# An AdaLN block on one core: both ends reworked, the modulation rows after the first projection, and a key-value product in halves

## The chip, the core and the metric

One core of a Trainium2 chip runs the whole program. The metric is device time in microseconds (us), lower is better. In the text TensorE does matmuls (PE in the profile, PEld for its weight loads), VectorE is DVE, ScalarE is ACT, GpSimd is POOL, and SyncE (SP) issues most of the DMA transfers. Each engine runs its own instructions in order and waits on semaphores.

## The reference

x is 2 x 2048 tokens of 256 values; c holds one conditioning row for each of the two batches.

```python
mod = (silu(c) @ wmod).reshape(2, 6, 1, 256)
sa, ca, ga, sb, cb, gb = (mod[:, i] for i in range(6))
ga = (2 * (ga >= 0) - 1) * maximum(abs(ga), 0.25)     # gb alike
h = layernorm(x) * (1 + ca) + sa
x = x + ga * linear_attention(h)     # 16 heads of 16: Q, K = elu(.) + 1
h = layernorm(x) * (1 + cb) + sb
x = x + gb * moe(h)                  # 8 experts, 256 -> 128 -> 256, gelu, top 2
```

Linear attention is Q (K^T V) / (Q sum K), then the output projection Wo and its bias bo. The router adds a cosine score to a linear one. All is fp32.

## The kernel before

Tokens are worked in 16 units (NU) of two tiles of 128 tokens; eight units make a batch. Two pipelines run over the units, each a `step_a` or `step_e` on every engine, with the same semaphores counted per unit.

**Attention pass (`step_a`).** VectorE makes the layer norm statistics (`stats_a`, three units ahead), GpSimd the reciprocal root (`rstd_a`), ScalarE normalises, TensorE transposes (`tp_a`, L720), ScalarE modulates by columns, VectorE rounds to the high half (`split_a`, L1052), GpSimd makes the low half (`split_lo`, L376). TensorE projects in three products of halves: `qk` (bias L739, then L708 to L710) for each tile, then `v`. ScalarE and VectorE form the feature map (`feature_map`, L1134), and TensorE adds K^T V for the unit before (`kv`, L774): for each half c of the 256 features a 128 x 128 fp32 product, of which only the 16 x 16 blocks of a head on the diagonal are used. VectorE adds it to `kv_acc` (`add_kv`, L1145). GpSimd sums K (`add_ksum`) and adds ga * bo to x (`add_bo`, L393). VectorE also splits a sixteenth of the expert weights in each unit (`split_weights`).

**Start.** Eight matmuls on TensorE (L793) give the modulation columns sa and ca. `mod_rows(b)` then gives ga, sb, cb, gb of batch b as rows spread over all 128 partitions, by a weight operand `c_rep` in which silu(c) is repeated 128 times: four fp32 matmuls of 512 columns, recorded as eight. Batch 0 comes ahead of the first projection, batch 1 after it. VectorE's `mod_rows(b)` clips the two gates (ten operations, L1100 to L1116), and `bias_o` forms ga * bo. On GpSimd, the centroid norm (`normalise_centroids`, L520) stands between the steps of unit 0 and 1, and needs VectorE's `clip_centroids`, which follows `mod_rows(1)`. SyncE issues all loads of x, W and small rows in one queue; from unit 4 on the x loads wait for the load two units before.

**Middle.** After eight units of a batch `mask_kv` (L1197, L1202) adds the value bias and masks K^T V to its diagonal blocks, `make_m` (L837) folds it into Wo, and `split_m` multiplies by ga. The expert pass starts while the last units of attention end.

**Expert pass (`step_e`).** For each unit four expert pairs p: TensorE `first(u, p)`, ScalarE gelu, VectorE `gate(u, p)` (L1279), ScalarE the high half (`hi_hid`, L664), GpSimd the low half (`lo_e`), or VectorE (`lo_hid`, L1286) in the last two units; then TensorE `second(u, p)` (its first instruction for p = 0 is L918) sums into bank 6. VectorE's `scale_experts(u)` (L1343) empties that bank, and the next unit's `second(u, 0)` waits for it (`e_yg`). In `step_e(u)` VectorE runs, in order, gate 0, 1, 2, then `scale_experts(u - 1)`, then gate 3. In the last unit, tile 1 sums into bank 7.

## Time and profile before

| | us |
|---|---|
| median of 3 runs (388.28 to 390.07) | 389.62 |
| the profiled execution | 390.11 |
| its span, first to last instruction | 388.40 |

| engine | busy us | share |
|---|---|---|
| TensorE | 355.6 | 92% |
| TensorE weight loads | 331.6 | 85% |
| VectorE | 294.5 | 76% |
| ScalarE | 229.2 | 59% |
| GpSimd | 283.7 | 73% |

The page cuts the span into 40 slices of 9.7 us. A digit is the busy share in tenths; PEclk is the clock granted to TensorE in tenths of full speed.

```profile
PE   4897999999997655999999999999999999999696
DVE  4889777777886877787887887887887887776443
POOL 3716899999976758689888888888888888765201
PEclk9999999999999966799999999999999999999899
```

A timeline row is: start in us from the span's start, duration, engine, line, operation, output<-inputs, shape, count, and in brackets the idle time of the engine before it and what ended that. Rows with a count over 1 are several instructions merged. Matmul ends are modelled, so that neighbouring durations overlap; from one start to the next is the better measure.

### The profile page before, as it was taken

The page shows a single profiled execution, that of the slowest core. Times are in us where ns is not written, and L with a number is a line of the kernel's source. Part 1 is how long each engine was busy: PE and PEld are TensorE (multiplying, and loading weights), DVE is VectorE, ACT ScalarE, POOL GpSimd, SP SyncE. Part 2 cuts the span into 40 slices and gives each one's busy share as a digit, 9 for nine tenths or more (in the row PEclk, how much of TensorE's full clock was granted, in tenths as well). Part 3 has the DMA queues.
Part 4 walks back from the last instruction along what each step waited for, and adds up shares of the span by engine and source line. Part 5 has one row for each costly group of instructions (what it writes and reads, how often), then busy time and mean ns, then how long its engine had stood idle before and what let it go on. Part 6 is the DMA issues. An engine that isn't in the chain of part 4 may idle for free.

```text
span 388.4 us, 8954 instructions
## 1 busy us (share of the span) xinstructions
PE 355.6 (92%) x2610; PEld 331.6 (85%) x2610; DVE 294.5 (76%) x833; ACT 229.2 (59%) x499; POOL 283.7 (73%) x389
## 2 busy tenths in 40 slices
PE   4897999999997655999999999999999999999696
PEld 4376889888896644999999999999999999999685
DVE  4889777777886877787887887887887887776443
ACT  2245778778773414765855855855855855773450
POOL 3716899999976758689888888888888888765201
PEclk9999999999999966799999999999999999999899
DMA  7954000000000002203224214214214214233301
GB/s 260 336 175 155 2 0 0 0 0 0 2 1 0 2 16 93 83 32 136 84 57 136 82 55 135 82 55 135 82 55 135 82 56 135 84 88 105 131 7 56
DMA packets 23147, 30.35 MB, mean 78 GB/s; under 512 B 2242, under 2 KB 13906, under 8 KB 23124
## 3 DMA queue, kind: packets, MB, share of 16 engines
q1 hardware_dynamic: 22308, 29.02, 23.8%
q10 hardware_dynamic: 816, 1.05, 0.8%
q8 instruction: 11, 0.18, 0.2%
q14 instruction: 12, 0.10, 0.1%
HBM read 25.74 MB, written 4.33 MB: 77 GB/s over the span
## 4 chain that ended last, share of the span: by engine, by line
PE 56%; POOL 7%; DVE 6%; issue 4%; ACT 2%; POOLq 0%; DVEq 0%
PE bank L708 17%; PE bank L710 16%; PE bank L709 16%; PE bank L716 3%; PE bank L880 2%; POOL x_sb L393 1%; PE bank L918 1%; POOL k_sum L386 1%; DVE hid_g L1279 1%; POOL tr_lo L376 1%; ACT hid_pair L664 1%; POOL early L424 1%; POOL early L434 1%; POOL rstd L360 1%; PE bank L837 1%
## 5 line engine op out<-in xcount | busy, mean ns | idle before, releaser
L657 ACT ACTIVATE bank<-bank,cols_sb 128x256 f32<-128x256 f32 x128 | 51.4, 439 | 50.6 <-PE bank L710 50.5
L461 POOL TENSOR_TENSOR hid_pair<-hid_g,hid_pair 128x512 fp32r<-128x512 f32 x56 | 72.4, 1293 | 6.9 <-ACT hid_pair L664 4.6
L708 PE MATMUL bank<-tr_hi,w_hi 128*128 128x256 f32 x256 | 74.4, 290 | 0.0
L710 PE MATMUL bank<-tr_hi,w_lo 128*128 128x256 f32 x256 | 72.9, 285 | 0.0
L709 PE MATMUL bank<-tr_lo,w_hi 128*128 128x256 f32 x256 | 72.8, 284 | 0.0
L708 PE MATMUL bank<-w_hi,hid_pair 128*128 128x256 f32 x252 | 70.9, 281 | 0.0
L709 PE MATMUL bank<-w_lo,hid_pair 128*128 128x256 f32 x252 | 70.9, 281 | 0.0
L710 PE MATMUL bank<-w_hi,hid_pair 128*128 128x256 f32 x252 | 70.9, 281 | 0.0
L664 ACT ACTIVATE hid_pair<-hid_g 128x512 fp32r<-128x512 f32 x64 | 40.4, 632 | 28.5 <-DVE hid_g L1279 27.1
L1279 DVE TENSOR_TENSOR hid_g<-bank,g_bc 128x512 f32<-128x512 f32 x64 | 43.7, 683 | 9.8 <-ACT bank L657 8.3
L708 PEld LDWEIGHTS bank<-tr_hi,w_hi 128*128 128x128 f32 x256 | 49.1, 192 | 0.2
L709 PEld LDWEIGHTS bank<-tr_lo,w_hi 128*128 128x128 f32 x256 | 49.1, 192 | 0.1
L710 PEld LDWEIGHTS bank<-tr_hi,w_lo 128*128 128x128 f32 x256 | 49.1, 192 | 0.0
L710 PEld LDWEIGHTS bank<-w_hi,hid_pair 128*128 128x128 f32 x252 | 48.2, 191 | 0.0
L709 PEld LDWEIGHTS bank<-w_lo,hid_pair 128*128 128x128 f32 x252 | 48.2, 191 | 0.0
L708 PEld LDWEIGHTS bank<-w_hi,hid_pair 128*128 128x128 f32 x252 | 48.1, 191 | 0.0
L710 PE MATMUL bank<-hid_pair,tr_lo 128*128 128x512 f32 (+1 forms) x128 | 43.7, 341 | 0.0
L708 PE MATMUL bank<-hid_pair,tr_hi 128*128 128x512 f32 (+1 forms) x128 | 43.5, 340 | 0.0
L709 PE MATMUL bank<-hid_pair,tr_hi 128*128 128x512 f32 (+1 forms) x128 | 43.5, 340 | 0.0
L577 ACT ACTIVATE e_sb<-bank 128x512 f32<-128x512 f32 x32 | 19.1, 597 | 27.3 <-PE bank L710 27.1
L1296 DVE STREAM_TRANSPOSE bank<-bank 32x64 f32<-32x64 f32 x64 | 16.6, 259 | 23.9 <-PE bank L880 23.2
L475 POOL TENSOR_TENSOR x_sb<-x_sb,k_sb 128x512 f32 (+1 forms) x15 | 19.6, 1303 | 16.6 <-DVE k_sb L1343 16.6
(152 smaller groups left out, 942.4 us busy)
## 6 DMA issues: line engine op xcount, KB each, us to landing
g_bc<-g_dram SPq DMA_DIRECT2D x64, 256.0 KB, 3.5
x_sb<-in_x SPq DMA_DIRECT2D x16, 256.0 KB, 2.9
out<-x_sb SPq DMA_DIRECT2D x15, 256.0 KB, 2.2
early<-in_wmod ACTq DMA_DIRECT2D x2, 512.0 KB, 8.1
q_sb<-in_w SPq DMA_DIRECT2D x2, 512.0 KB, 6.2
q_sb<-in_w SPq DMA_DIRECT2D x1, 1024.0 KB, 9.1
...
```

What stands on the lines that cost most here:

```text
L461: gp.tensor_tensor(hid_lo[:, p, :, :], hid_g[:, p % 2, :, :], hid_hi[:, p, :, :].bitcast(F32), ALU.subtract).then_inc(e_hlo, 1)
L475: gp.tensor_tensor(xt, xt, y_g[:, :, :], ALU.add).then_inc(e_y, 1)
L577: ac.activation(e_sb[:, t, :], bank[2 + t][:, :], ACT.Relu, scale=-1.0).then_inc(a_neg, 1)
L657: last = ac.activation(half, half, ACT.Gelu, bias=b1_sb[:, e:e + 1])
L664: ac.activation(hid_hi[:, p, :, :].rearrange("p j n -> p (j n)"), hid_g[:, p % 2, :, :].rearrange("p j n -> p (j n)"), ACT.Copy).then_inc( ...
L708: te.matmul(out_ap, l_hi, r_hi, start=start, stop=False, skip_group_check=shared)
L709: te.matmul(out_ap, l_hi, r_lo, start=False, stop=False, skip_group_check=shared)
L710: return te.matmul(out_ap, l_lo, r_hi, start=False, stop=stop, skip_group_check=shared)
L716: last = te.transpose(dst[:, c, t * P:(t + 1) * P], of[:, t, c * P:(c + 1) * P], ident[:, :])
L880: last = te.matmul(lgT, route_r[:, c, :], part[:, h, c, :], start=(c == 0 and k == 0), stop=(c == NC - 1 and k == 1))
L1279: TT(hid_g[:, s, :, :].rearrange("p j n -> p (j n)"), bank[2 + p][:, :], g_bc[:, p, :, :].rearrange("p j n -> p (j n)"), ALU.mult).then_in ...
L1296: last = ve.transpose(lg[32 * q:32 * (q + 1), :, :], by_quarter[:, :, q, :])
```

## The change

- **Modulation rows.** silu(c) itself, two columns, is the weight operand, so that both batches come at once in two partitions. `mod_rows(0)` and `mod_rows(1)` are now the two halves of the columns (ga, sb and cb, gb), both behind `step_a` of unit 0 on TensorE. VectorE clips the gates once, on two partitions, after its step of unit 0, and forms ga * bo there. SyncE waits for it, stores five rows of each batch to DRAM, waits, and reads them back to all partitions. GpSimd's first `add_bo` and VectorE's first `mask_kv` wait for that. TensorE's matmul for bo is gone.
- **Loads.** The last two parts of wmod are issued by SyncE ahead of x of unit 2; the small rows by ScalarE.
- **Who splits what.** The high half of Wq, Wk, Wv is made by ScalarE; the low half of unit 0 by VectorE; the bias rows are split by GpSimd (`split_bqk`), before the reciprocal root of unit 1.
- **GpSimd's order.** `normalise_centroids` comes after the step of unit 2. VectorE's `split_b2` and `split_route` move from unit 1 to unit 3.
- **Key-value product.** Only the two 64 x 64 blocks on the diagonal of each 128 x 128 are formed: eight matmuls of 64 weight columns by 64, in place of four of 128 by 128. `kv_acc` and the masking shrink to match; `kv_m` is cleared once.
- **End.** In the last two units `scale_experts(u - 1)` moves ahead of `gate(u, 2)`; the last unit sums into banks 0 and 7 and does not wait for `e_yg`.

The diff, without declarations:

```diff
@@ -252,7 +254,7 @@
 
         def sums(u, t):
 
-            return bank[7][:, 0:E] if t == 1 and u.nth(NU - 1) else bank[6][:, t * E:(t + 1) * E]
+            return bank[7 * t][:, 0:E] if u.nth(NU - 1) else bank[6][:, t * E:(t + 1) * E]
 
         def kv_bank(u):
             return bank[2] if u.nth(NU - 1) else bank[6 + u.h]
@@ -275,21 +277,28 @@
 
             x_tiles = x.rearrange("(t p) e -> p t e", p=P)
             out_tiles = out.rearrange("(t p) e -> p t e", p=P)
-            small = [(rows_raw[0:1, :], rows), (rows_raw[32:33, :], rows), (cols_sb[:, :], cols),
-                     (b2_raw[:, :], b2)]
-            assert len(small) == N_SMALL
+            def load_wmod(k):
+                cols_k = slice(k * 2 * E, (k + 1) * 2 * E)
+                sp.dma_start(wmod_sb[:, :, cols_k], wmod_chunks[:, :, cols_k]).then_inc(d_wmod[k], 16)
+
             load_x(0, 0)
-            sp.dma_start(wmod_sb[:, :, 0:2 * E], wmod_chunks[:, :, 0:2 * E]).then_inc(d_wmod[0], 16)
+            load_wmod(0)
             sp.dma_start(wqkv_raw[:, :, :], wqkvT.rearrange("(c p) n -> p c n", p=P)).then_inc(d_qkv, 16)
             load_x(0, 1)
-            for to, of in small:
-                sp.dma_start(to, of).then_inc(d_small, 16)
+            load_wmod(1)
+            load_wmod(2)
             load_x(1, 0)
             load_x(1, 1)
             sp.dma_start(w1_raw[:, 0, :, :], w1[:, 0:P, :].rearrange("e p j -> p e j")).then_inc(d_w, 16)
             sp.dma_start(w1_raw[:, 1, :, :], w1[:, P:2 * P, :].rearrange("e p j -> p e j")).then_inc(d_w, 16)
             sp.dma_start(w2_raw, w2.rearrange("e p d -> p e d")).then_inc(d_w, 16)
             sp.dma_start(wo_sb[:, :, :], woT.rearrange("(c p) n -> p c n", p=P)).then_inc(d_wo, 16)
+
+            sp.wait_ge(modrow_ready, 1)
+            sp.dma_start(mod_dram[:, 0:4, :], mod_of).then_inc(mod_put, 16)
+            sp.dma_start(mod_dram[:, 4, :], ga_bo).then_inc(mod_put, 16)
+            sp.wait_ge(mod_put, 32)
+            sp.dma_start(mod_row[:, :, :, :], mod_dram.partition_broadcast(P)).then_inc(mod_got, 16)
             with sp.Fori(2, NU // 2) as it:
                 for h in range(2):
@@ -402,14 +411,27 @@
                     add_ksum(u.plus(-1))
                 if u.nth(2):
 
-                    pool.wait_ge(ga_bo_ready, B)
+                    pool.wait_ge(mod_got, 16)
                 if u.plus(-2) and not u.plus(-2).nth(NU - 4) and not u.plus(-2).nth(NU - 3):
                     add_bo(u.plus(-2))
 
+            def split_bqk():
+
+                pool.wait_ge(d_small, 16 * N_SMALL)
+                pool.wait_ge(zero_rows, 1)
+                pool.wait_ge(a_rstd, 1)
+                gp.tensor_copy(bqk_t[32:33, :], bqk_raw[32:33, :]).then_inc(bqk_step, 1)
+                pool.wait_ge(bqk_step, 1)
+                gp.tensor_copy(bqk_r[0:1, :], bqk_raw[0:1, :]).then_inc(bqk_step, 1)
+                pool.wait_ge(bqk_step, 2)
+                gp.tensor_tensor(bqk_r[32:33, :], bqk_raw[32:33, :], bqk_t[32:33, :].bitcast(F32), ALU.subtract)\
+                  .then_inc(bqk_ready, 1)
+                pool.wait_ge(bqk_ready, 1)
+
             u0 = unit(0)
             rstd_a(u0)
+            split_bqk()
             rstd_a(u0.plus(1))
-            split_lo(u0)
 
             def make_prod(u):
 
@@ -520,8 +542,10 @@
                 gp.tensor_tensor(cent_rn[:, :], cent_n2[:, :], minus_half[:, :], ALU.pow).then_inc(cent_ready, 1)
 
             step_a(u0)
+            step_a(unit(1))
+            step_a(unit(2))
             normalise_centroids()
-            pipeline(gp, step_a, 1, 2, NU - 4, NU - 2)
+            pipeline(gp, step_a, 3, 4, NU - 4, NU - 2)
 
             pool.wait_ge(f_ksrow, 1)
             gp.memset(prod[:, :, D:D + 1], DEN_EPS)
@@ -548,9 +572,11 @@
 
             act.wait_ge(d_c, 16)
             ac.activation(c_exp[:, :, :], c_sb[:, :, :], ACT.Exp, scale=-1.0).then_inc(c_exp_ready, 1)
-            for k in range(1, 3):
-                cols_k = slice(k * 2 * E, (k + 1) * 2 * E)
-                act.dma_start(wmod_sb[:, :, cols_k], wmod_chunks[:, :, cols_k]).then_inc(d_wmod[k], 16)
+            small = [(bqk_raw[0:1, :], rows[:, 0:2 * E]), (bqk_raw[32:33, :], rows[:, 0:2 * E]),
+                     (bo_raw, rows[0, 2 * E:3 * E].partition_broadcast(B)), (cols_sb[:, :], cols), (b2_raw, b2[0:NE, :])]
+            assert len(small) == N_SMALL
+            for to, of in small:
+                act.dma_start(to, of).then_inc(d_small, 16)
 
             def normalise(u):
 
@@ -602,6 +628,10 @@
 
             u0 = unit(0)
             normalise(u0)
+
+            act.wait_ge(d_qkv, 16)
+            for c in range(NC):
+                ac.activation(wqkv_hi[:, c, :], wqkv_raw[:, c, :], ACT.Copy).then_inc(qkv_step, 1)
 
             act.wait_ge(modcol_ready, 1)
             modulate(u0, 0)
@@ -746,9 +776,6 @@
                 h = u.h
 
                 wait(pe, a_vs, u.count(1, -1))
-                if u.nth(0):
-
-                    pe.wait_ge(bo_ready, 1)
                 if u.nth(1):
 
                     pe.wait_ge(cent_n2_ready, 1)
@@ -767,12 +794,13 @@
                 wait(pe, a_acc, u.count(1, 0))
                 if u.nth(0):
 
-                    pe.wait_ge(modrow_step, MODROW_STEPS * B)
+                    pe.wait_ge(modrow_ready, 1)
                 for c in range(NC):
-                    f = slice(c * P, (c + 1) * P)
                     for t in range(2):
-                        last = te.matmul(kv_bank(u)[:, f], v_sb[:, h, t, f], k_sb[:, h, t, f],
-                                         start=(t == 0), stop=(t == 1))
+                        for half in HALVES:
+                            f = slice(c * P + half, c * P + half + 64)
+                            last = te.matmul(kv_bank(u)[half:half + 64, c * 64:(c + 1) * 64], v_sb[:, h, t, f],
+                                             k_sb[:, h, t, f], start=(t == 0), stop=(t == 1))
                 last.then_inc(a_kv, 1)
 
             def step_a(u):
@@ -797,26 +825,19 @@
             pe.wait_ge(const_ready, 1)
             tp_a(u0)
 
-            def mod_rows(b):
-
-                wait(pe, modrow_step, MODROW_STEPS * b)
-                for k in range(2):
-                    pe.wait_ge(d_wmod[1 + k], 16)
-                    for c in range(NC):
-                        last = te.matmul(bank[6 + k][:, :], c_rep[:, c, b, :],
-                                         wmod_sb[:, c, 2 * E * (k + 1):2 * E * (k + 2)],
-                                         start=(c == 0), stop=(c == NC - 1))
+            def mod_rows(k):
+
+                pe.wait_ge(d_wmod[1 + k], 16)
+                for c in range(NC):
+                    last = te.matmul(bank[6 + k][0:B, :], c_silu[:, c, :], wmod_sb[:, c, 2 * E * (k + 1):2 * E * (k + 2)],
+                                     start=(c == 0), stop=(c == NC - 1))
                 last.then_inc(modrow_done, 1)
 
-            mod_rows(0)
-
-            pe.wait_ge(d_small, 16 * N_SMALL)
             pe.wait_ge(ones_ready, 1)
-            te.matmul(bank[4][:, 0:E], ones_f[0:1, :], bo_raw[0:1, :], start=True, stop=True).then_inc(bo_done, 1)
-
             pe.wait_ge(qkv_ready, 1)
             pe.wait_ge(bqk_ready, 1)
             step_a(u0)
+            mod_rows(0)
             mod_rows(1)
 
             pe.wait_ge(cent_sq_ready, 1)
@@ -910,7 +931,8 @@
 
                     wait(pe, e_gTr, u.count(1, 1))
                     wait(pe, e_gThi2, u.count(1, 1))
-                    wait(pe, e_yg, u.count(1, 0))
+                    if not u.nth(NU - 1):
+                        wait(pe, e_yg, u.count(1, 0))
                 for t in range(2):
                     tok = slice(t * P, (t + 1) * P)
                     to = sums(u, t)
             stats_a(u0.plus(1))
-
-            dve.wait_ge(d_qkv, 16)
-            for c in range(NC):
-                ve.tensor_copy(wqkv_hi[:, c, :], wqkv_raw[:, c, :]).then_inc(qkv_step, 1)
 
             dve.wait_ge(modcol_done, 1)
             mc = bank[5][:, 0:4 * B].rearrange("p (k b) -> p k b", b=B)
@@ -1056,23 +1069,19 @@
                 last = TT(wqkv_lo[:, c, :], wqkv_raw[:, c, :], wqkv_hi[:, c, :].bitcast(F32), ALU.subtract)
             last.then_inc(qkv_ready, 1)
             split_a(u0)
+            dve.wait_ge(a_hi, 1)
+            TT(tr_lo[:, 0, :, :], tr_f[:, 0, :, :], tr_hi[:, 0, :, :].bitcast(F32), ALU.subtract).then_inc(a_lo, 1)
 
             dve.wait_ge(d_small, 16 * N_SMALL)
-            dve.wait_ge(zero_rows, 1)
-            ve.tensor_copy(bqk_t[32:33, :], bqk_raw[32:33, :]).then_inc(bqk_step, 1)
-            ve.tensor_copy(bqk_r[0:1, :], bqk_raw[0:1, :])
-            dve.wait_ge(bqk_step, 1)
-            TT(bqk_r[32:33, :], bqk_raw[32:33, :], bqk_t[32:33, :].bitcast(F32), ALU.subtract).then_inc(bqk_ready, 1)
-
             TT(cent_sq[:, :, :], route_raw[:, :, 0:NE], route_raw[:, :, 0:NE], ALU.mult).then_inc(cent_sq_ready, 1)
 
             def split_b2():
 
-                ve.tensor_copy(b2_r[0:NE, :], b2_raw[0:NE, :])
-                ve.tensor_copy(b2_r[32:32 + NE, :], b2_raw[0:NE, :])
-                ve.tensor_copy(b2_t, b2_raw[0:NE, :]).then_inc(b2_split, 1)
+                ve.tensor_copy(b2_r[0:NE, :], b2_raw)
+                ve.tensor_copy(b2_r[32:32 + NE, :], b2_raw)
...
+                dve.wait_ge(modrow_done, 2)
+                ga, shift_b = (bank[6][0:B, k * E:(k + 1) * E] for k in range(2))
+                cb, gb = (bank[7][0:B, k * E:(k + 1) * E] for k in range(2))
+                ve.tensor_copy(mod_of[:, 1, :], shift_b)
+                ve.tensor_scalar(mod_of[:, 2, :], cb, 1.0, None, ALU.add)
                 both = ((0, ga), (1, gb))
                 for i, src in both:
+                    last = ve.tensor_scalar(gate_sign[:, i, :], src, 0.0, 2.0, ALU.is_ge, ALU.mult)
                 last.then_inc(modrow_step, 1)
+                dve.wait_ge(modrow_step, 1)
                 for i, src in both:
+                    last = ve.scalar_tensor_tensor(gate_abs[:, i, :], gate_sign[:, i, :], -1.0, src, ALU.add, ALU.mult)
                 last.then_inc(modrow_step, 1)
...
@@ -1164,26 +1165,20 @@
                     split_a(u.plus(1))
                 feature_map(u, 0)
                 feature_map(u, 1)
-                for b in range(B):
-                    if u.nth(b):
-
-                        split_weights(u)
-                        bias_o(b)
-                if u.nth(1):
+                if u.nth(0) or u.nth(1):
+
+                    split_weights(u)
+                if u.nth(3):
                     split_b2()
                     split_route()
                 if u.plus(3):
                     stats_a(u.plus(3))
 
             stats_a(unit(2))
-
-            dve.wait_ge(bo_done, 1)
-            ve.tensor_copy(bo_sb, bank[4][:, 0:E]).then_inc(bo_ready, 1)
-            mod_rows(0)
             step_a(u0)
-            mod_rows(1)
+            mod_rows()
             clip_centroids()
-            pipeline(ve, step_a, 1, 2, NU - 4, NU - 3)
+            pipeline(ve, step_a, 1, 4, NU - 4, NU - 3)
 
             def mask_kv(b, sums):
 
@@ -1194,12 +1189,17 @@
 
                 wait(dve, f_m, b)
                 for c in range(NC):
-                    last = ve.scalar_tensor_tensor(kv_b[:, c, :], ksum_row[:, b, c * P:(c + 1) * P],
-                                                   bv_sb[:, c:c + 1], kv_acc[:, b, c, :], ALU.mult, ALU.add)
+                    for half in HALVES:
+                        rows = slice(half, half + 64)
+                        last = ve.scalar_tensor_tensor(kv_b[rows, c, :],
+                                                       ksum_row[rows, b, c * P + half:c * P + half + 64],
+                                                       bv_sb[rows, c:c + 1], kv_acc[rows, b, c, :], ALU.mult, ALU.add)
                 last.then_inc(f_step, 1)
                 dve.wait_ge(f_step, 2 * b + 1)
-                for c in range(NC):
-                    last = TT(kv_m[:, c, :], kv_b[:, c, :], head_mask[:, :], ALU.mult)
+                for half in HALVES:
+                    rows = slice(half, half + 64)
+                    mask = head_mask[rows, half:half + 64].rearrange("p (o n) -> p o n", o=1).to_broadcast([64, NC, 64])
+                    last = TT(kv_m[rows, :, half:half + 64], kv_b[rows, :, :], mask, ALU.mult)
                 last.then_inc(f_kvm, 1)
 
             def split_m(b, product):
@@ -1371,11 +1371,13 @@
                     add_attention(u.plus(3))
                 if u.nth(-1):
                     split_m(1, bank[4])
+                if at_end(u):
+                    scale_experts(u.plus(-1))
                 if u:
                     gate(u, 2)
                 if at_end(u):
                     lo_hid(u, 2)
-                if u.plus(-1):
+                elif u.plus(-1):
                     scale_experts(u.plus(-1))
                 if u.plus(3):
                     stats_e(u.plus(3))
@@ -1386,6 +1388,8 @@
                 if u.plus(2):
                     lo_e(u.plus(2))
 
+            dve.wait_ge(mod_got, 16)
+            ve.memset(kv_m[:, :, :], 0.0)
             mask_kv(0, bank[0][:, 0:E])
 
             step_a(unit(NU - 3))
```

## Rows read from the trace of the kernel before

**Rows 1.** Stages: stretch, its us, busy us of each engine, clock, DMA share, GB/s.

```profile
40.60:97.20 56.60, 56.60 (x365) 50.46 (x365) 41.83 (x114) 44.66 (x86) 52.09 (x76) 1.00 0.00 0
...
364.80:368.20 3.40, 3.40 (x18) 3.40 (x17) 0.84 (x2) 0.63 (x1) 0.99 (x1) 0.50 0.39 131
```

**Rows 2.** Timeline, TensorE, start: start us, us, instruction, idle before it.

```profile
11.41 6.29 PE L806 MATMUL bank<-early,g_bc 128*128 128x512 f32 x8 [1.09 <-DMA early<-in_wmod]
...
18.25 0.50 PE L739 MATMUL bank<-bqk_r,ones_r 128*128 128x512 f32 x1
...
23.48 3.60 PE L806 MATMUL bank<-early,g_bc 128*128 128x512 f32 x8
...
35.77 0.49 PE L739 MATMUL bank<-bqk_r,ones_r 128*128 128x512 f32 x1 [2.24 <-POOL tr_lo L376]
...
43.31 0.48 PE L739 MATMUL bank<-bqk_r,ones_r 128*128 128x512 f32 x1
```

**Rows 3.** Timeline, TensorE, attention loop.

```profile
60.47 1.06 PE L774 MATMUL bank<-k_sb,v_sb 128*128 128x128 f32 x8
61.28 0.48 PE L739 MATMUL bank<-bqk_r,ones_r 128*128 128x512 f32 x1
```

**Rows 4.** Timeline, GpSimd, attention loop.

```profile
45.67 0.23 POOL L357 TENSOR_SCALAR neg_mean<-mv 128x2 f32<-128x2 f32 x1
...
51.75 0.23 POOL L357 TENSOR_SCALAR neg_mean<-mv 128x2 f32<-128x2 f32 x1
```

**Rows 5.** Timelines, GpSimd (first three) and VectorE, start.

```profile
14.52 1.81 POOL L376 TENSOR_TENSOR tr_lo<-tr_f,tr_hi 128x512 fp32r<-128x512 f32 x1
...
30.80 1.86 POOL L520 TENSOR_TENSOR cent_rn<-cent_n,minus_half 128x8 f32<-128x8 f32 x1 [6.87 <-DVE cent_n L1080]
...
41.44 1.29 POOL L376 TENSOR_TENSOR tr_lo<-tr_f,tr_hi 128x512 fp32r<-128x512 f32 x1
...
27.11 0.42 DVE L1100 COPY mod_row<-bank 128x256 f32<-128x256 f32 x1 [0.79 <-PE bank L806]
...
29.89 0.76 DVE L1116 SCALAR_TENSOR_TENSOR mod_row<-q_sb 128x256 f32<-128x256 f32 x2
...
38.09 0.75 DVE L1009 BATCH_NORM_STATS2 stats<-x_sb 128x6 f32<-128x256 f32 x2
```

**Rows 6.** Timeline, VectorE, end.

```profile
360.97 0.69 DVE L1286 TENSOR_TENSOR hid_pair<-hid_g,hid_pair 128x512 fp32r<-128x512 f32 x1 [0.85 <-ACT hid_pair L664]
...
363.67 0.68 DVE L1343 TENSOR_TENSOR k_sb<-bank,mod_row 128x512 f32<-128x512 f32 x1
```

**Rows 7.** Timeline, TensorE, end.

```profile
364.50 0.35 PE L918 MATMUL bank<-b_r,gT_r 128*128 128x256 f32 x1 [3.06 <-DVE k_sb L1343]
...
378.71 0.36 PE L918 MATMUL bank<-b_r,gT_r 128*128 128x256 f32 x1 [0.92 <-DVE k_sb L1343]
```

**Rows 8.** Timeline, SyncE: a store to DRAM and the reads that wait for it.

```profile
142.25 0.31 SPq L306 DMA_DIRECT2D g_dram<-gT_f  x1
143.56 1.77 SPq L313 DMA_DIRECT2D g_bc<-g_dram  x4
```

**Rows 9.** A stretch of those reads, columns as in rows 1.

```profile
146.00:147.00 1.00, 1.00 (x5) 0.91 (x5) 0.76 (x3) 0.61 (x4) 0.20 (x1) 0.50 1.00 383
```

**Rows 10.** Page, DMA issues: count, KB each, median us to landing.

```profile
x_sb<-in_x SPq DMA_DIRECT2D x16, 256.0 KB, 2.9
```

**Rows 11.** Groups, weight loads by form: count, busy us, mean ns, idle before.

```profile
L774 PEld LDWEIGHTS bank<-k_sb,v_sb 128*128 128x128 f32 x128 | 15.6, 191 | 0.0
...
L880 PEld LDWEIGHTS bank<-tr_lo,route_r 128*32 128x32 f32 x32 | 3.5, 108 | 0.2
```

**Rows 12.** Timeline, TensorE, expert loop: last router matmul and the next.

```profile
180.32 0.28 PE L880 MATMUL bank<-tr_lo,route_r 128*32 128x256 f32 x1
180.44 0.27 PE L708 MATMUL bank<-tr_hi,w_hi 128*128 128x256 f32 x1
```

**Rows 13.** Timeline, VectorE, masking of the second batch.

```profile
142.56 1.14 DVE L1197 SCALAR_TENSOR_TENSOR early<-ksum_row,cols_sb,kv_acc 128x128 f32<-128x128 f32 x2
```

76 lines of the change are left out of this document (30 added, 46 removed).

## The prediction

> **What bounds the kernel now.** I read the page first (busy shares, clock by slices), then the stretches with their clock, then the engines' timelines at both ends, since the diff works there. The reader should see three stages.
>
> In the attention loop TensorE is busy for the whole of 56.6 us at full clock [rows 1]; three units from 43.31 to 61.28 give 5.99 us each [rows 2, 3]. GpSimd is hardly freer: one of its steps, with nothing waited for, goes from 45.67 to 51.75, 6.08 us [rows 4]. The expert loop is TensorE's as well, and the diff leaves it alone.
>
> At the start the first projection begins at 18.25, because TensorE first does eight modulation matmuls in 6.29 us; the same eight take 3.60 us at 23.48 [rows 2]. GpSimd idles 6.87 us for the centroid norm, which VectorE clips only after the second modulation chain. That makes the split of unit 2 late, and TensorE idles 2.24 us before 35.77 [rows 2, 5]. The unit after it takes 43.31 - 35.77 = 7.54 us, not 5.99.
>
> At the end TensorE idles 3.06 us before 364.50, until VectorE has scaled the experts of the unit before (363.67), an operation queued behind a gate and a split of the current unit; then 3.4 us pass at 0.50 of the clock, the lower of its levels, 1.2 GHz. It idles 0.92 us before 378.71 for the same kind of operation [rows 1, 6, 7].
>
> **The tail.** The scaling moves ahead of the third gate. VectorE's split in front ends at 360.97 + 0.69 = 361.66, so the scaling ends at 362.3 where it ended at 364.35; TensorE starts at 362.5, 2.0 us earlier [rows 6, 7]. The idle left is 1.1 us, far below the 3.06 that preceded the low clock, so I count the low clock gone: half of 3.4 us, 1.7 us. For the last unit the sums go to two free banks and no scaling is awaited: 0.9 us [rows 7]. The last unit's third gate and split now stand behind its scaling and move back by an estimated 1.2 us, to 379.2 on the old scale; TensorE, with 26 matmuls at 0.11 us before it, comes to them at 377.8 + 2.9 = 380.7. What is late next is TensorE itself. Sum -4.6 us; if the low clock stays, -2.9.
>
> **The start.** Removed from TensorE: one of two modulation sets and the bias broadcast. Moved behind the first projection: what is left, 3.5 us. The casts go to ScalarE, the first low half to VectorE (0.69, the like split at 360.97 [rows 6]) from GpSimd, where it ended at 14.52 + 1.81 = 16.33 [rows 5]. The bias rows take its place on GpSimd: three operations, each at most the 1.29 of the low-half split at 41.44 [rows 5], which has as many elements a partition, so up to 3.9 us, after small transfers whose landing no row fixes. Bounds of the first projection: 13 (all inputs early) and 17.5 (transfers late); I take 14. Unit 0 took 23.48 - 18.25 = 5.2 us at full clock [rows 2]. Now nothing runs before it, and at the lower clock it would take twice that; I take the middle, 7.8, so it ends at 21.8 (20.5 to 24.5). The modulation matmuls end at 25.3 and unit 1 starts at 25.7.
>
> VectorE's modulation chain took 3.5 us, from 27.11 to 30.65 [rows 5]. It is now one chain, on two partitions, with one product more: 3.8 us, ready at 29.2. TensorE's first key-value step waits for it, at 30.8: hidden.
>
> **The new wait.** SyncE waits for that chain, and behind this wait are queued the two stores of the rows, the read of 1.31 MB to all partitions, and every load of x from unit 4 on, all on one queue. A store to its waiter takes 143.56 - 142.25 = 1.31 us [rows 8]; two, 1.7. 1.31 MB at 383 GB/s [rows 9] takes 3.4 us, and an x load alone 2.9 [rows 10], plus 0.45 of issue. So x of unit 4 lands at 29.2 + 0.1 + 1.7 + 0.45 + 3.4 + 2.9 = 37.7. VectorE's statistics of unit 4 wait for it, and behind them on VectorE stands the split of unit 3; GpSimd takes their result before the low half of unit 3. Before, the statistics began at 38.09, and that low half was ready at 41.44 + 1.29 = 42.73 [rows 5]: 4.64 us. After: 37.7 + 4.6 = 42.3. TensorE, no longer stalled at unit 2, is through with it at 25.7 + 12 = 37.7 and idles 4.7 us. It starts unit 3 at 42.5 instead of 43.31 [rows 2], but now the low clock follows, at a price like 7.54 - 5.99 = 1.6 us, where before it had been paid by then. Unit 4 begins at 42.5 + 6.0 + 1.6 = 50.1 against 49.3: **+0.8 us**. The whole front rework is eaten by the queue. Bounds: that load earlier or later by 2.5 us (start, chain and transfer each off), with a longer or no low clock: -3 to +4.
>
> **The loop.** Per unit the key-value product was 4 fp32 matmuls of 128 weight columns by 128, recorded as eight: 61.28 - 60.47 = 0.81 us [rows 3]. Now it is 8 of 64 by 64, sixteen records. Each streams half the columns, so equal streaming if nothing overlaps, 0.8; weight loads take 191 ns for 128 columns and 108 for 32 [rows 11], 0.87 ns a column, so sixteen of 64 columns stream in 0.9 us, eight of 128 in the same. The row nearest by shape, the 32-column router load, speaks for this scaling: I take no change. Ends: 0.4 us if the two halves overlap, 1.8 if a load-matmul pair costs 0.11 whatever its size. The low end brings nearly nothing in the loop, because GpSimd's 6.08 binds [rows 4]; the high end is +0.9 us a unit. VectorE's accumulation halves its 256 columns: hidden behind TensorE. **0 us**, from -1 to +11.
>
> The Trainium skill, page TensorEngine Tiling (Array Packing), section Key Properties, says that changing the tiling mode drains TensorE. The trace does not agree: the router's four matmuls are such a change, and the step from 180.32 (128 rows by 32 columns) to 180.44 (128 by 128) is 0.12 us, no more than inside either group [rows 12]. By the page the loop would be longer by what rival (d) gives; by the row it is not.
>
> **The middle.** TensorE waited for the masking of the second batch's key-value matrix: two operations of 128 columns in 1.14 us [rows 13]. Now four of 64 columns on half the partitions; from 0.7 to 1.3 us in all; I take 0.8. With shorter accumulations on VectorE's chain there, **-0.6 us** (-1 to +0.5). The new clearing (0.3 us) falls on the first batch, where TensorE has work.
>
> **Sum.** +0.8 + 0 - 0.6 - 4.6 = -4.4. The profiled execution took 390.11 (span 388.40 and 1.71 around it), 0.5 above the median 389.62; so 385.7 or 385.2: I forecast **385.4**.
>
> **Rivals.**
> (a) Main: tail gain whole, front about even: 384 to 387.5. Chance 0.50.
> (b) The front gains too: x of unit 4 lands by 35, TensorE idles about 2 us or loses no clock. Then unit 4 begins some 3 us sooner: 382. For it: the bounds above. 0.15.
> (c) The front loses: the transfers or the start are late by 2.5 us, so GpSimd and TensorE shift by as much: 388.5. 0.12.
> (d) Each change of the array's shape, two a unit, waits for the matmul in flight: 0.28 less the usual 0.12 [rows 12], 0.3 us a unit over 11 units, +3.5; or the pairs take 0.075 us (+0.4 a unit): 389 to 390, no change. Against it: the router's step and the columns' scaling [rows 11, 12]. 0.13.
> (e) Slower: the pair has a fixed floor of 0.11 us, no row showing one closer. It decides from 1.45 us a unit on, where +0.6 over 11 units outweighs the 4.4 us and the 2 of measuring; at 1.8 it gives 385.4 + 10 = 395. Against it: the column scaling. 0.10.
> That the tail does nothing (low clock stays, next wait 1 us behind) is inside (a) to (c): +1.7.
>
> **Chances and range.** About 0.5% (2 us) is what a measurement here can tell from no change. Faster by more: (a), (b) and a third of (c): 0.69. Within: the rest of (c), and (d): 0.21. Slower: (e), 0.10. The range from 381.5 to 391.5 holds (a) to (d) but their ends, and leaves (e) out.
>
> **What would show it.** Tail: TensorE's idle before the unit-14 second product about 1 us, no low clock after it, none before the last unit's. Front: first projection at 14, TensorE idle before unit 3 for about 5 us, released by the chain x load, statistics, GpSimd. Loop: the key-value records 0.8 to 0.9 us, the unit 5.99. I am wrong if the key-value group takes over 1.2 us a unit, or the x load lands outside 35 to 40.

## The result, and the profile after

The changed kernel takes 392.12 us (median of four runs, 390.41 to 392.53), the kernel before beside it 389.4 (388.28 to 390.07). The ratio is 1.0076, with a 95% interval of 1.005 to 1.0101: about 3 us slower. The forecast was 385.4, in a range of 381.5 to 391.5; the time is outside it, and on the other side of no change. The profiled execution took 390.41, the quickest of the four; its span is 388.7.

From the page of the kernel after: the engines, then the granted clock in 40 slices of 9.7 us:

```profile
PE 350.2 (90%) x2728; PEld 324.9 (84%) x2728; DVE 289.7 (75%) x818; ACT 230.2 (59%) x501; POOL 283.3 (73%) x391
PEclk9999699999999975699999999999999999999999
```

TensorE is 5.4 us less busy than before, yet the span is the same. PEclk shows what has moved: before it dipped in the middle and in the third slice from the end, now in the fifth slice (the start) and the middle, and no more at the end.

The timeline of TensorE in the kernel after (start us, us, instruction, in brackets the idle before it and its releaser):

```profile
14.77 0.77 PE L769 MATMUL bank<-bqk_r,ones_r 128*128 128x512 f32 x1 [4.62 <-DVE tr_lo L1073]
...
42.49 0.79 PE L769 MATMUL bank<-bqk_r,ones_r 128*128 128x512 f32 x1 [5.27 <-POOL tr_lo L385]
51.14 0.49 PE L769 MATMUL bank<-bqk_r,ones_r 128*128 128x512 f32 x1
58.99 0.49 PE L769 MATMUL bank<-bqk_r,ones_r 128*128 128x512 f32 x1 [1.85 <-POOL tr_lo L385]
65.01 0.49 PE L769 MATMUL bank<-bqk_r,ones_r 128*128 128x512 f32 x1
...
143.74 0.39 PE L738 MATMUL bank<-m_hi,qz_hi 128*128 128x256 f32 x1 [2.31 <-DVE qz_lo L1228]
...
148.37 2.07 PE L858 MATMUL bank<-wo_sb,early 128*128 128x256 f32 x4 [1.91 <-DVE early L1202]
...
367.55 0.36 PE L940 MATMUL bank<-b_r,gT_r 128*128 128x256 f32 x1 [0.98 <-DVE k_sb L1343]
```

L769 is the bias row that opens a unit's projection (before, L739). Units 0 and 3 to 6 start at 14.77, 42.49, 51.14, 58.99 and 65.01; before, units 0, 3 and 6 start at 18.25, 43.31 and 61.28 [rows 2, 3]. So the front is 0.8 us ahead at unit 3 and **3.7 us behind at unit 6**. At the end, the wait of 3.06 us is 0.98 and the one of 0.92 is gone [rows 7].

The stretch of unit 3 (stretch, its us; busy us and instructions of TensorE, its weight loads, VectorE, ScalarE, GpSimd; granted clock, DMA share, GB/s):

```profile
42.49:51.14 8.65, 8.65 (x46) 7.14 (x47) 3.49 (x8) 4.47 (x9) 8.05 (x11) 0.66 0.62 185
```

Unit 3 takes 8.65 us instead of 5.99, because the granted clock is at its lower level, 1.2 GHz, in most of it. Unit 4 takes 7.85 us: 6.00 of work and 1.85 of idle. The last 34 us, from 355.00 on, run at full clock, 1.00.

The stretches add up. Unit 6 starts 3.73 us later than before, from there to the first expert product (L940, before L918) it is 0.68 longer, from that to unit 13's 0.70 longer, and the end is 4.81 shorter: +0.30, the difference of the two spans. The second of these terms is the least certain, as the lower clock falls differently in the middle of the kernel: it is 102.04 us here and 101.13 in the trace of after_again, the same kernel. There unit 6 starts at 66.30, 5.0 us behind the kernel before.

What TensorE waited for, link by link. SyncE's queue, then VectorE, then GpSimd, kernel after:

```profile
28.81 0.32 SPq L298 DMA_DIRECT2D mod_dram<-g_bc  x1
...
30.41 0.35 SPq L301 DMA_DIRECT2D mod_row<-mod_dram  x1
31.17 13.07 SPq L276 DMA_DIRECT2D x_sb<-in_x  x7
```
```profile
37.75 0.75 DVE L1031 BATCH_NORM_STATS2 stats<-x_sb 128x6 f32<-128x256 f32 x2 [5.27 <-DMA x_sb<-in_x]
...
51.18 0.48 DVE L1080 CAST b_r<-g_bc 8x256 fp32r<-8x256 f32 x1
...
54.29 0.74 DVE L1031 BATCH_NORM_STATS2 stats<-x_sb 128x6 f32<-128x256 f32 x2
...
146.03 1.66 DVE L1194 SCALAR_TENSOR_TENSOR early<-ksum_row,cols_sb,kv_acc 64x64 f32<-64x64 f32 x4
147.73 0.58 DVE L1202 TENSOR_TENSOR early<-early,head_mask 64x128 f32<-64x128 f32 x2
```
```profile
38.95 0.37 POOL L366 TENSOR_SCALAR neg_mean<-mv 128x2 f32<-128x2 f32 x1 [6.74 <-DVE mv L1037]
...
55.68 0.23 POOL L366 TENSOR_SCALAR neg_mean<-mv 128x2 f32<-128x2 f32 x1 [2.85 <-DVE mv L1037]
```

The first chain is the forecast's: modulation rows at 28.8, two stores, the spread at 30.41, the x load of unit 4 behind it, its data at 37.75 (forecast 37.7). The second one stands in no line of the prediction: from 51.18 to 54.29 VectorE splits the experts' output bias b2 and the router's weights (L1080 to L1101), and only then makes the statistics of unit 6, for which GpSimd has idled 2.85 us. The diff moved these splits from unit 1 to unit 3. Their results are wanted late: the first router product (L901) is at 137.54, the first product with b2 (L940) at 167.05.

### The profile page after: what moved, and what is told of

Same layout as the page of the kernel before. It is cut to its first block, busy times and chain, and to the rows that moved or that the text cites. A ratio compares the mean times of both kernels' runs of the same rounds, so it can differ in the third digit from the quotient of the medians.

```text
span 388.7 us, 9135 instructions
## 1 busy us (share of the span) xinstructions
PE 350.2 (90%) x2728; PEld 324.9 (84%) x2728; DVE 289.7 (75%) x818; ACT 230.2 (59%) x501; POOL 283.3 (73%) x391
## 4 chain that ended last, share of the span: by engine, by line
PE 57%; POOL 6%; DVE 5%; issue 4%; ACT 1%; POOLq 0%; DVEq 0%
PE bank L738 17%; PE bank L740 16%; PE bank L739 16%; PE bank L746 3%; PE bank L901 2%; POOL x_sb L402 1%; PE bank L940 1%; POOL k_sum L395 1%; POOL tr_lo L385 1%; POOL early L446 1%; POOL early L456 1%; POOL rstd L369 1%; PE bank L858 1%; DVE den L1221 1%; DVE early L1194 0%
## 5 line engine op out<-in xcount | busy, mean ns | idle before, releaser
L739 PE MATMUL bank<-tr_lo,w_hi 128*128 128x256 f32 x256 | 73.0, 285 | 0.0
L739 PE MATMUL bank<-w_lo,hid_pair 128*128 128x256 f32 x252 | 70.1, 278 | 0.0
L739 PEld LDWEIGHTS bank<-tr_lo,w_hi 128*128 128x128 f32 x256 | 49.4, 193 | 0.1
L740 PEld LDWEIGHTS bank<-w_hi,hid_pair 128*128 128x128 f32 x252 | 47.5, 188 | 0.0
L739 PEld LDWEIGHTS bank<-w_lo,hid_pair 128*128 128x128 f32 x252 | 47.5, 188 | 0.0
L738 PEld LDWEIGHTS bank<-w_hi,hid_pair 128*128 128x128 f32 x252 | 47.4, 188 | 0.0
L738 PE MATMUL bank<-hid_pair,tr_hi 128*128 128x512 f32 (+1 forms) x128 | 44.5, 348 | 0.0
L739 PE MATMUL bank<-hid_pair,tr_hi 128*128 128x512 f32 (+1 forms) x128 | 44.3, 346 | 0.0
L1031 DVE BATCH_NORM_STATS2 stats<-x_sb 128x6 f32 (+1 forms) x64 | 23.8, 413 | 9.9 <-DMA x_sb<-in_x 9.9
```

The source lines that it names most:

```text
L738: te.matmul(out_ap, l_hi, r_hi, start=start, stop=False, skip_group_check=shared)
L739: te.matmul(out_ap, l_hi, r_lo, start=False, stop=False, skip_group_check=shared)
L740: return te.matmul(out_ap, l_lo, r_hi, start=False, stop=stop, skip_group_check=shared)
L1031: last = ve.bn_stats(stats[:, h, t, :], x_sb[:, u.tile(t), :])
```

## The experiments

All ratios are against the kernel before, on the same chip.

| kernel | us, median | ratio, 95% interval | us against before |
|---|---|---|---|
| tail_only | 384.18 | 0.9886 (0.9858 to 0.9913) | -4.4 |
| kv_only | 389.05 | 1.0004 (0.9983 to 1.0024) | +0.2 |
| front_only | 395.04 | 1.0154 (1.0126 to 1.0182) | +6.0 |
| after_again | 390.98 | 1.0057 (1.0034 to 1.0081) | +2.2 |
| x_first | 385.77 | 0.9917 (0.9888 to 0.9946) | -3.2 |
| stats_first | 389.41 | 1.0008 (0.9993 to 1.0022) | +0.3 |
| bo_late | 392.44 | 1.0089 (1.0065 to 1.0112) | +3.5 |
| both | 383.44 | 0.9855 (0.9831 to 0.9879) | -5.6 |
| both_kv_full | 382.79 | 0.9836 (0.9809 to 0.9863) | -6.4 |
| both_cent | 382.42 | 0.9823 (0.9797 to 0.9848) | -6.9 |
| both_tail_off | 388.76 | 0.9995 (0.9978 to 1.0012) | -0.2 |
| best | 381.39 | 0.9815 (0.9791 to 0.9838) | -7.2 |

The last column is (ratio - 1) x 389.

### The three parts, each alone

**tail_only**: the kernel before with the hunks of `sums`, of the wait for `e_yg`, and of `scale_experts` in `step_e`.

> The kernel before with only the three edits at its end (scaling ahead of the third gate in the last two units, the last unit's sums in two free banks, no wait for the scaling there). Theory 1, the forecast's tail: both stalls (3.06 and 0.92 us) nearly go and the low clock at the end with them, so 4.0 to 4.8 us less than before, about 385. Rival 2, the tail gains only part, because the low clock comes anyway: 2.5 to 3 us less, about 386.8, with a stretch at half clock after 355 us. Rival 3, the tail gave nothing and the changed kernel is slower for that reason: 389.

4.4 us less. The last 34 us of its timeline and its stretch:

```profile
361.21 0.36 PE L919 MATMUL bank<-b_r,gT_r 128*128 128x256 f32 x1 [0.99 <-DVE k_sb L1344]
348.10:382.30 34.20, 29.46 (x250) 29.09 (x250) 18.79 (x43) 13.72 (x31) 8.69 (x9) 1.00 0.28 85
```

One wait of 0.99 us is left and the clock is 1.00. Theory 1 holds, rivals 2 and 3 fall.

**kv_only**: the kernel before with the halves in `kv`, `kv_acc`, `add_kv` and `mask_kv`, and the clearing.

> The kernel before with only the key-value product in halves (and what holds it: accumulation, bias, mask, clearing). Theory 1: the product falls from 0.81 to 0.6 or 0.7 us a unit, but GpSimd's 6.08 us step binds the loop, so 0 to 1 us less, 388.5 to 389.5; TensorE idles for GpSimd a little in the loop. Rival 2 (a change of the array's shape costs, rival (d) of the prediction): 0.3 us a unit more, 392 to 393. Rival 3 (the middle: masking in four operations and the clearing stand in TensorE's way): up to 1 us more, seen before the first product with the masked matrix.

No difference (+0.2 us, interval -0.7 to +0.9). Six units of its loop:

```profile
61.06:96.68 35.62, 35.61 (x281) 30.11 (x277) 27.24 (x73) 28.39 (x55) 32.67 (x49) 1.00 0.00 0
```

A unit takes 35.62 / 6 = 5.94 us where it took 5.99. TensorE counts as busy for 35.61 of 35.62 us, but that hides short waits, since a matmul's end is modelled and reaches past the next start. The starts show them. First the kernel after, around the key-value group ahead of unit 6 (the later part of the group alone, then GpSimd's low half that unit 6 needs); then the like group in x_first, the run below with the same product:

```profile
64.09 0.28 PE L740 MATMUL bank<-hid_pair,tr_lo 128*128 128x256 f32 x1
64.30 0.69 PE L802 MATMUL bank<-k_sb,v_sb 128*64 128x64 f32 x16
65.01 0.49 PE L769 MATMUL bank<-bqk_r,ones_r 128*128 128x512 f32 x1
...
64.52 0.46 PE L802 MATMUL bank<-k_sb,v_sb 128*64 128x64 f32 x10
...
63.59 1.29 POOL L385 TENSOR_TENSOR tr_lo<-tr_f,tr_hi 128x512 fp32r<-128x512 f32 x1
```
```profile
60.18 0.28 PE L742 MATMUL bank<-hid_pair,tr_lo 128*128 128x256 f32 x1
60.38 0.69 PE L804 MATMUL bank<-k_sb,v_sb 128*64 128x64 f32 x16
61.00 0.50 PE L771 MATMUL bank<-bqk_r,ones_r 128*128 128x512 f32 x1
...
59.32 1.29 POOL L387 TENSOR_TENSOR tr_lo<-tr_f,tr_hi 128x512 fp32r<-128x512 f32 x1 [1.07 <-DVE tr_hi L1067]
```

In x_first the low half is ready at 60.61, well ahead, and the group with its edges takes 61.00 - 60.18 = 0.82 us. In the trace of before the last projection matmul starts at 60.35, so there it took 61.28 - 60.35 = 0.93. TensorE alone thus gains 0.11 us a unit (its next two units in x_first take 5.93 and 5.89 us). In the kernel after, the low half ends at 63.59 + 1.29 = 64.88 and TensorE starts 0.13 later. At the long stall before unit 3 it is the same 0.13 (41.09 + 1.27 = 42.36, start at 42.49). So here TensorE waits for GpSimd, 0.1 us that no bracket shows, and the whole takes 65.01 - 64.09 = 0.92. In kv_only the starts are 0.13 or 0.14 us behind the low half in five of the six units, and the low halves come 5.96 us apart. Theory 1 holds with its reason: GpSimd's pace takes about half of what TensorE gains. Rival 2, 0.3 us a unit more, falls.

Why the gain is 0.11 and not more: ten records from 64.52 end at 64.98, a record lasts 0.22, so the last starts at 64.76, and four steps take 0.24: a *pair* of records starts every 0.06 us, where a full-width record took 0.81 / 8 = 0.10 [rows 3]. The two halves run side by side, and eight pairs at that rate would be 0.48 us. From the group's first record to the next unit it is 61.00 - 60.38 = 0.62, and the step into the group is 0.20 to 0.21 instead of the usual 0.12. So the edges cost some 0.09 us going in and 0.14 inside and going out. In the Trainium skill, page TensorEngine Tiling (Array Packing), section Key Properties, this is two rules: different tiles can load and multiply in parallel, and a change of the tiling mode drains TensorE. This trace agrees with both.

The masking shows the third part, rival 3: in kv_only the four operations (L1202) take 1.67 us where two took 1.14 [rows 13], and TensorE idles 1.70 us before the product with the masked matrix.

**front_only**: the kernel after with its tail and its key-value product as before.

> The changed kernel with tail and key-value product put back as before, so the rework of the start alone. Theory 1: all of the loss lies here: TensorE idles about 5 us before unit 3 (x of unit 4 behind the rows' round trip), then 6.8 us at half clock, then a stall at unit 5 for the router's split ahead of the statistics; +3.7 at unit 6 or later, 393.0 to 396.5 in all, by how much low clock follows. Rival 2 (front even, as forecast at +0.8; the loss comes from key-value halves): 389.5 to 391.

6.0 us more: theory 1, rival 2 falls. Its TensorE, and ten microseconds from unit 5 on:

```profile
43.17 0.49 PE L768 MATMUL bank<-bqk_r,ones_r 128*128 128x512 f32 x1 [4.33 <-POOL tr_lo L384]
59.41 0.49 PE L768 MATMUL bank<-bqk_r,ones_r 128*128 128x512 f32 x1 [2.15 <-POOL tr_lo L384]
59.00:69.00 10.00, 9.59 (x48) 8.18 (x49) 6.34 (x17) 5.78 (x12) 8.82 (x14) 0.83 0.00 0
```

Two stalls, and here a low clock behind the second one too: 0.83 on average, which is 3.4 us of the ten at half speed, 1.7 us lost. In the profiled run of the kernel after that second dip was missing (its stall was 1.85 us, not 2.15), while the first was longer: 5.9 us of unit 3 at half speed, against 3.4 us between 42 and 52 us here and in after_again.

**after_again**: the changed kernel, unchanged.

> The changed kernel once more, beside the three partial ones. The parts should add: with theory 1, before + front (+3.7 to +7) + halves (0 to -1) + tail (-4.6) = 389 to 392; 391 to 392.5 by the runs so far. Rival: the parts don't add, since a stall that one part takes out at the end comes back as low clock elsewhere; then tail alone gains over 1 us more than what is missing from the sum.

+2.2 us, and the parts add: 6.0 - 4.4 + 0.2 = 1.8. The rival falls. Its profiled run, of 390.62 us, has the second dip (0.83 on average from 59 to 69 us), behind this stall:

```profile
58.85 0.49 PE L769 MATMUL bank<-bqk_r,ones_r 128*128 128x512 f32 x1 [2.38 <-POOL tr_lo L385]
```

### The two stalls of the start

**x_first**: the loads of x for two units ahead of the wait.

```diff
+            load_x(2, 0)
+            load_x(2, 1)
             sp.wait_ge(modrow_ready, 1)
...
-            with sp.Fori(2, NU // 2) as it:
+            with sp.Fori(3, NU // 2) as it:
```

> The changed kernel (391 to 392) with the loads of x for units 4 and 5 issued ahead of SyncE's wait for the modulation rows. Theory 1 (the queue behind that wait is the cause at unit 3): x of unit 4 lands by 30 instead of 37.7, TensorE's idle of 5.3 us before unit 3 and the low clock after it go; the stall before unit 5 (the router's split ahead of the statistics) stays or grows, so 4 to 6.5 us less than the changed kernel: 384.5 to 387.5. Rival 2 (GpSimd's wait for the rows, 37.0 us, is as late and takes over): the idle only moves to unit 4, 1 to 2 us less: 389.5 to 390.5.

-3.2 us, so 5.4 less than after_again: theory 1. TensorE:

```profile
45.30 0.49 PE L771 MATMUL bank<-bqk_r,ones_r 128*128 128x512 f32 x1 [1.21 <-POOL tr_lo L387]
53.62 0.79 PE L771 MATMUL bank<-bqk_r,ones_r 128*128 128x512 f32 x1 [2.32 <-POOL tr_lo L387]
```

The two loads are issued from 15.28 on instead of 31.17. Unit 3 has no idle before it; unit 4 waits 1.21 us and unit 5, behind the moved splits, 2.32, followed by a low clock (the matmul takes 0.79, not 0.49).

**stats_first**: the statistics of unit 6 ahead of the moved splits.

```diff
+                if u.plus(3):
+                    stats_a(u.plus(3))
                 if u.nth(3):
                     split_b2()
                     split_route()
-                if u.plus(3):
-                    stats_a(u.plus(3))
```

> The changed kernel with the router's and the output bias' splits (3.2 us on VectorE in unit 3) behind the statistics of unit 6 instead of ahead of them. Theory 1 (that order is the cause of the stall of 1.85 us before unit 5): the stall goes, and with it the second stretch of low clock that the runs of over 391 us show: 1.9 to 3.5 us less than the changed kernel, 387.5 to 389.5. Rival 2 (GpSimd with its centroid root and its backlog is the cause): 0 to 0.5 us less.

+0.3, so 1.9 us less than after_again, at the low end of theory 1. TensorE and GpSimd:

```profile
58.96 0.50 PE L769 MATMUL bank<-bqk_r,ones_r 128*128 128x512 f32 x1 [1.35 <-POOL tr_lo L385]
...
57.56 1.27 POOL L385 TENSOR_TENSOR tr_lo<-tr_f,tr_hi 128x512 fp32r<-128x512 f32 x1 [1.62 <-DVE tr_hi L1065]
```

The stall before unit 5 is 1.35 us and not gone; the clock behind it, from 59 to 69 us, stays at 1.00. So the order on VectorE made some 0.5 to 1 us of that stall, and with it the low clock. What is left has the same cause: GpSimd has its statistics in time, and idles 1.62 us for VectorE's high half of unit 5 (L1065, 57.06), which is queued behind the same splits, now from 52.70 to 55.73. The edit took one reader out from behind the block and left the next one there. Rival 2, GpSimd's own backlog, isn't what holds this unit. No run has the splits in a place where no engine is behind them.

**bo_late**: GpSimd's wait for the spread rows one step later.

```diff
-                if u.nth(2):
+                if u.nth(3):
                     pool.wait_ge(mod_got, 16)
+                    add_bo(u0)
```

> The changed kernel with GpSimd's wait for the spread rows and its first addition of the output bias moved from its step 2 to its step 3. Theory 1 (x of unit 4 is what holds unit 3): no change within 0.5 us, TensorE still starts unit 3 at 42.5 to 43. Rival 2 (GpSimd's wait for the rows holds it): unit 3 starts over 1 us earlier and the kernel gains 1 to 3 us.

```profile
44.20 0.79 PE L770 MATMUL bank<-bqk_r,ones_r 128*128 128x512 f32 x1 [5.64 <-POOL tr_lo L385]
60.65 0.66 PE L770 MATMUL bank<-bqk_r,ones_r 128*128 128x512 f32 x1 [3.22 <-POOL tr_lo L385]
```

The stall before unit 3 is as long as ever, so rival 2 falls: the rows' landing is not what holds it. Theory 1 said no change, though, and by the ratios it is 1.2 us worse (3.46 against 2.22), each good to about 0.9; the stall before unit 5 is 3.22 instead of 2.38. GpSimd's two additions in one step (52.47 to 55.09) aren't the cause: behind them it still idles 2.24 us for VectorE's statistics, behind the splits, which took 4.4 us here (51.51 to 55.95) and 3.1 to 3.9 in the two traces of the changed kernel. Why they took longer stays open.

**both**: x_first and stats_first together.

> The changed kernel with both edits, x of units 4 and 5 ahead of the wait and the statistics ahead of the router's split. Theory 1 (these two are the whole of the front's loss): the gains add or more, unit 6 begins by 57 to 60 us against 65.0 in the changed kernel and 61.28 before; 380 to 384.5 in all, below the kernel with the tail alone (384.2) or level with it. Rival 2 (something third binds, GpSimd with the rows' landing or its extra work): no better than 385.5.

-5.6 us: 7.8 less than after_again, where the two gave 5.4 and 1.9 alone. Theory 1: unit 6 begins at 58.26.

```profile
45.42 0.50 PE L771 MATMUL bank<-bqk_r,ones_r 128*128 128x512 f32 x1 [1.24 <-POOL tr_lo L387]
52.38 0.49 PE L771 MATMUL bank<-bqk_r,ones_r 128*128 128x512 f32 x1 [1.01 <-POOL tr_lo L387]
```

No low clock is left in the start, since neither stall is long.

### What is left

**both_tail_off**: both, with the tail as before.

> The kernel with both front edits, its end put back as before: the repaired start and the halves without the tail. Theory 1: the start, repaired, gains about 1 us against the kernel before where as changed it lost 6; 387 to 388.3, and the tail is again worth 4 to 4.8 us. Rival 2 (parts don't add): the repaired start gains over 2 us by itself, under 386.7.

-0.2 us, so the repaired start by itself is no gain that can be told, less than the 1 us expected, and rival 2 falls. Beside both the tail is worth 5.4 us, above the 4 to 4.8 expected; each ratio is good to about 1 us, and between the two traces the end, from unit 13's product on, differs by 4.84.

**both_kv_full**: both, with the key-value product in full width.

> The kernel with both front edits (383.4), but the key-value product, accumulation and mask in full width as before. Theory 1: halves save 0.05 us a unit where GpSimd binds and cost 0.6 us in the masking of batch 1 (four operations of 0.42 us for two of 0.57); so no difference that can be told, 383 to 384.5, and TensorE waits 1.1 us instead of 1.7 before the product with the masked matrix. It also asks why the expert loop is 0.6 to 0.7 us longer in every kernel with both start and halves: theory 1 has no answer, if it stays longer here the start is the cause. Rival 2 (halves gain once the start is repaired and TensorE is the bound): 1 us or more longer, 384.5 to 386.

-6.4, 0.7 us less than both, within the two intervals, and just below the range of theory 1. Rival 2 falls: the halves gain nothing. TensorE's wait before the product with the masked matrix is 1.80 us, not the 1.1 expected, because part of the work before it ran at full clock in this trace. From the start of that work to the product it is 4.01 us, as in tail_only; with the halves, in the kernel both, 4.64.

The expert loop, from its first unit to unit 13, takes 186.82 us here and 187.40 in the kernel both. It was so in every kernel that had the new start and the halves (187.28 to 187.42), and in none with only one of them (186.7 to 186.8). The product that opens expert unit 2 (L942, L940) shows where, first in the kernel both, then in both_kv_full, each with VectorE's scaling of the experts that it waits for:

```profile
189.34 0.60 PE L748 MATMUL bank<-ident,nat 128*128 128x128 f32 x4
189.89 0.36 PE L942 MATMUL bank<-b_r,gT_r 128*128 128x256 f32 x1
...
189.06 0.68 DVE L1345 TENSOR_TENSOR k_sb<-bank,mod_row 128x512 f32<-128x512 f32 x1
```
```profile
189.41 0.60 PE L747 MATMUL bank<-ident,nat 128*128 128x128 f32 x4
189.76 0.37 PE L940 MATMUL bank<-b_r,gT_r 128*128 128x256 f32 x1
...
188.76 0.68 DVE L1338 TENSOR_TENSOR k_sb<-bank,mod_row 128x512 f32<-128x512 f32 x1
```

In the kernel both the scaling ends at 189.74 and TensorE starts 0.15 later, the same 0.15 as at the end of the kernel before (363.67 + 0.68 = 364.35, start at 364.50 [rows 6, 7]). In both_kv_full it ends 0.32 ahead, and TensorE goes on at once. So it is the tail's wait again, in the middle of the loop: up to 0.19 us at units 2, 4, 6 and 8, hidden from the busy time by the modelled ends. What makes VectorE later in these kernels stays open: neither edit changes the work of an instruction in that loop.

**both_cent**: both, with the centroid norm in an earlier idle time of GpSimd.

```diff
+            for c in range(NC):
+                last = te.matmul(bank[5][:, 0:NE], ones_f, cent_sq[:, c, :], start=(c == 0), stop=(c == NC - 1))
             mod_rows(0)
             mod_rows(1)
...
+            clip_centroids()
             mod_rows()
-            clip_centroids()
...
             step_a(u0)
+            normalise_centroids()
             step_a(unit(1))
             step_a(unit(2))
-            normalise_centroids()
```

> The kernel with both front edits (383.4), and the centroid norm moved into an idle time of GpSimd: its two small matmuls ahead of the modulation rows on TensorE, the clip ahead of the modulation chain on VectorE, the root (1.7 us) ahead of GpSimd's step 1. Theory 1 (GpSimd's backlog of steps 2 and 3 is what is left of the front's stalls, 1.24 us before unit 4 and 1.01 us before unit 5): both stalls shrink to under 0.5 us in sum, 1 to 2 us less: 381.5 to 382.7. Rival 2 (the landing of x or the rows holds it): no gain, 383.4.

-6.9, 1.3 us less than both (with overlapping intervals). The time is in theory 1's range, at the lower end of its gain; the stalls aren't, 1.47 us in sum where under 0.5 was expected.

The stall before unit 4 is gone, so that one was GpSimd's centroid root (1.71 us in the kernel both, at 40.68). The one before unit 5 (52.40) is 1.47, as TensorE reaches it sooner. It isn't GpSimd's backlog: GpSimd idles 1.63 us before the low half of unit 5, for VectorE's high half behind the moved splits (45.98 to 49.17).

**best**: both_cent with the full-width product.

> The kernel with the moved centroid norm (382.4), its key-value product and mask put back in full width. Theory 1 (the halves cost 0.6 us in the masking and go with 0.65 us more in the expert loop, and save 0.05 us a unit in the attention loop): 0 to 1.2 us less, 381.2 to 382.4, with 186.7 us from the first expert unit to unit 13 instead of 187.4. Rival 2 (with GpSimd's backlog gone, the halves' shorter product pays in the loop): 0.3 to 1 us more, 382.7 to 383.4.

381.39 us, ratio 0.9815: 1.85% faster than the kernel before, and some 2.5% faster than the changed one. Theory 1 holds. The attention loop keeps one stall, of 1.05 us before unit 5 (51.31), and the expert loop has its 186.7 us again (158.75 to 345.42).

## Why the prediction was wrong

| term | forecast us | measured us | from |
|---|---|---|---|
| tail | -4.6 | -4.4 | tail_only |
| start, to unit 4 | +0.8 | +1.2 to +1.8 | 50.52 to 51.14 against 49.3 (three traces) |
| start, units 4 and 5 | 0 | +1.9; +3.8 to +4.0 where a low clock follows | the same traces |
| start in all | +0.8 | +6.0 | front_only |
| loop | 0 | -0.05 a unit | kv_only |
| middle | -0.6 | +0.6 | 4.63 against 4.01, see below |
| expert loop | not in the sum | +0.6 | both, both_kv_full |

The three traces are those of the kernel after, after_again and front_only.

**The tail was right**, each step of it: 0.98 us left before the unit-14 product, no low clock behind it, no wait before the last unit. What came next was TensorE itself, as said. Between the traces of before and tail_only the end is 4.84 us shorter.

**The start's first half was right in mechanism**: first projection at 14.77 (forecast 14), x of unit 4 at 37.75 (37.7), unit 3 at 42.49 (42.5), idle 5.27 (4.7), and x_first shows that this queue was the cause. One size was off, and not in every run. For the low clock I took 1.6 us, the surplus of the stretch before [rows 2]. In the profiled run of the kernel after, unit 3 took 8.65 - 5.99 = 2.66 more. Its granted clock was 0.66 on average, which is 8.65 x 0.34 x 2 = 5.9 us at half speed; in the earlier stretch, before the change, it was 3.4 us. That is the 1.0 us there. In after_again the low clock took 3.4 us and the same unit 7.56 - 5.99 = 1.6 more, as forecast.

**The start's second half failed, and it is the step that decides**: "Unit 4 begins at 50.1 against 49.3: +0.8" was taken for the whole front. The diff shows `split_b2` and `split_route` leave unit 1 and enter unit 3, still ahead of the statistics. I followed what left (the stall before unit 2) and not where it went: 3.1 us on VectorE (51.18 to 54.29) at a moment when GpSimd had no lead, having just been held back by the late x. GpSimd got also the centroid root, 1.65 us behind its step 2. So a second stall of 1.85 to 2.4 us, and in two of the three traces a second low clock. front_only has the sum: 6.0 us instead of 0.8. Rival (c), "the front loses", had the sign and 2.5 us of it, and looked for it in the transfers, which were punctual.

**The loop's zero was nearly right, in part by luck.** I priced the halves at equal streaming (no overlap) and at no drain. The overlap is nearly full (a pair every 0.06 us) and the edges cost some 0.2, so that TensorE alone gains 0.11 us a unit. That is on the way to the low end that the prediction named, and its reason was right too: GpSimd's pace takes about half of it. Only the size of that pace was read from one step of 6.08 us [rows 4]; over five units of kv_only it is 5.96. I set the Trainium skill's rule on draining aside for the router's row of 0.12 us [rows 12]. That row tells nothing of this group: the router's product uses fewer columns of the array, but nothing runs beside it. The row that I needed, two groups of output partitions in use at once, wasn't in the trace of before. Rival (d), 0.3 us a unit, had most of the edges' cost, some 0.2, without the larger gain against it. Rival (e), a floor of 0.11 us a pair, falls: a pair takes 0.06.

**The middle had the wrong sign.** I took 0.8 us for the adding of the bias, which had taken 1.14 and now takes 1.67; with the mask behind it, 2.25 instead of 1.14 + 0.49 = 1.63. An operation of 64 x 64 lasts 0.42 us, one of 128 x 128 lasts 1.14 / 2 = 0.57 [rows 13]: a quarter of the elements, half as many in each partition, three quarters of the time. Cutting two into four adds. TensorE waits behind it. Its idle time alone misleads, as it depends on the clock of the work ahead (1.70 to 2.92 us in the kernels with halves); from the start of that work to the product with the masked matrix it is 148.37 - 143.74 = 4.63 us in the kernel after, and 143.56 - 139.55 = 4.01 with the old masking. First the masking of the kernel before on VectorE, then TensorE in tail_only:

```profile
143.73 0.49 DVE L1202 TENSOR_TENSOR early<-early,head_mask 128x128 f32<-128x128 f32 x2
```
```profile
139.55 0.58 PE L708 MATMUL bank<-m_hi,qz_hi 128*128 128x256 f32 x1 [3.74 <-DVE qz_lo L1229]
...
143.56 2.07 PE L837 MATMUL bank<-wo_sb,early 128*128 128x256 f32 x4 [1.09 <-DVE early L1203]
```

The Trainium skill, page VectorE: DVE Perf Modes, section The TRN2 errata, says that an operation from SBUF pays a fixed latency per instruction. These two durations, 0.42 and 0.57 us, agree.

Put together, with 11 units of the loop: 6.0 - 0.5 + 0.6 + 0.6 - 4.4 = +2.3 us, where -4.4 was forecast and +2.2 (after_again) and +3.0 were measured.

The chances were wrong too: 0.69 for faster rested on a tail that was sure and a front whose far end was +4, drawn from the start, the chain and the transfers alone. A moved block of 3 us on a busy engine belonged in it.
